# One block for attention and its inputs, and key and query loads in 12 transfers in place of 20

## The reference, cut to what matters

```python
h = layernorm(x) * (1 + ca) + sa                   # ca, sa: rows of silu(c) @ wmod
Xn = (h - mu) * rsqrt(var + 1e-5) * ln_g + ln_b
Q, K, V = split_heads(Xn @ Wq + bq), split_heads(Xn @ Wk + bk), split_heads(Xn @ Wv + bv)
A = softmax(where(causal, Q K^T / 4, -inf))        # 16 heads of 16 channels, 512 tokens
x = x + ga * ((A V) @ Wo + bo)
```

## Time and profile before

| | |
|---|---|
| median of 3 runs | 1178.86 us (1175.69 to 1179.64) |
| the profiled execution, its own time | 1173.97 us |
| its span, first to last instruction | 1171.9 us |
| mean granted TensorE clock | 0.897 |
| first attention scores / last attention values | 118.4 us / 362.0 us |
| busy share TensorE, VectorE, ScalarE, GpSimd | 81%, 63%, 56%, 39% |

### The profile page before, as it was taken

The page is one execution under the profiler, slowest core; times in us unless marked ns, Lnnn a source line. Parts: engine busy times, 40 slices in busy tenths (PEclk is TensorE's granted clock), DMA queues, the critical chain, the costliest instruction groups (busy, mean ns, idle before and its releaser), DMA issues. The chain is left out here.

```text
span 1171.9 us, 21496 instructions
## 1 busy us (share of the span) xinstructions
PE 954.3 (81%) x5454; PEld 796.3 (68%) x5454; DVE 742.1 (63%) x1917; ACT 652.3 (56%) x1693; POOL 456.9 (39%) x637
## 2 busy tenths in 40 slices
PE   6671999999997767969999970689699974999992
PEld 2461788888886655758999960468487753888882
DVE  4870798999994676468555535996447773444444
ACT  3562898999993345458666642579533322333331
POOL 3373564666662177603444443576301121010000
PEclk9786898999998787979999995799899986999997
DMA  7066443343322522447343429310042203000004
GB/s 247 17 222 212 114 102 90 91 90 90 90 54 64 180 100 101 153 150 251 124 128 121 126 98 303 99 45 1 14 143 75 72 28 127 24 31 33 28 15 152
DMA packets 112107, 123.15 MB, mean 105 GB/s; under 512 B 46720, under 2 KB 85120, under 8 KB 111896
## 3 DMA queue, kind: packets, MB, share of 16 engines
q1 hardware_dynamic: 102584, 97.89, 28.4%
q0 software_dynamic: 8608, 23.20, 5.3%
q10 hardware_dynamic: 832, 1.05, 0.3%
HBM read 77.73 MB, written 44.35 MB: 104 GB/s over the span
## 5 line engine op out<-in xcount | busy, mean ns | idle before, releaser
L717 ACT ACTIVATE PR<-PS,nmax 128x128 f32<-128x128 f32 (+3 forms) x256 | 135.7, 553 | 9.7 <-DVE nmax L758 8.4
L758 DVE TENSOR_REDUCE nmax<-PS 128x1 f32<-128x128 f32 (+3 forms) x256 | 113.5, 481 | 42.4 <-PE PS L661 37.0
L635 POOL TENSOR_SCALAR PR<-PR,rinv 128x128 f32<-128x128 f32 (+3 forms) x256 | 132.3, 537 | 0.0
L1355 POOL DMA_INDIRECT r_results<-r_y,r_to x79 | 75.9, 961 | 111.8 <-DVE r_to L1410 76.8
L660 PE MATMUL PS<-K,Q 128*128 128x128 f32 (+3 forms) x256 | 84.6, 390 | 30.4 <-PEq L138 26.4
L766 DVE TENSOR_TENSOR PTlo<-PS,PThi 128x512 fp32r<-128x512 f32 (+1 forms) x192 | 103.0, 590 | 2.9 <-ACT PThi L727 2.9
L727 ACT ACTIVATE PThi<-PS 128x512 fp32r<-128x512 f32 (+1 forms) x192 | 97.0, 547 | 6.7 <-PE PS L673 6.7
L673 PE MATMUL PS<-ident,PR 128*128 128x128 f32 x640 | 86.7, 281 | 3.6 <-DVE PTlo L766 3.0
L689 PE MATMUL PS<-PThi,V 128*128 128x512 f32 (+3 forms) x256 | 85.3, 346 | 1.1 <-DVE PTlo L766 0.5
L2350 DVE TENSOR_TENSOR x_h<-PS,x_sg 128x256 f32<-128x256 f32 x68 | 28.9, 424 | 86.4 <-ACT x_sg L2304 86.4
L2304 ACT ACTIVATE x_sg<-PS 128x256 f32<-128x256 f32 x68 | 26.2, 385 | 95.2 <-PE PS L2444 95.2
(11 more groups left out here) (374 smaller groups left out, 3067.8 us busy)
## 6 DMA issues: line engine op xcount, KB each, us to landing
r_xg<-r_sorted SPq DMA_DIRECT2D x79, 129.0 KB
r_wst<-in_routed SPq DMA_DIRECT2D x16, 608.0 KB, 5.3
K<-k_parts SPq DMA_DIRECT2D x120, 64.0 KB, 1.8
v_parts<-vp SPq DMA_DIRECT2D x4, 1024.0 KB, 7.5
V<-v_parts SPq DMA_DIRECT2D x64, 64.0 KB, 2.1
mlp_st<-r_results SPq DMA_DIRECT2D x8, 512.0 KB, 7.9
c_yg<-r_results SPq DMA_DIRECT2D x8, 512.0 KB
mlp_st<-in_up SPq DMA_DIRECT2D x8, 512.0 KB, 3.7
```

Source lines behind the costliest of these rows:

```text
L635: pool.tensor_scalar(PR[:, e % 4, i, 0:w], PR[:, e % 4, i, 0:w], rinv[:, e % 4, i:i + 1], 1.0, ALU.mult, ALU.mult).then_inc(norm_done, 1)
L717: act.activation(PR[:, e % 4, i, 0:w], k.PS[:, i, 0:w], ACT.Exp, bias=nmax[:, e % 4, i:i + 1], accum_out=rsum[:, e % 4, i:i + 1]).then_inc ...
L758: dve.tensor_reduce(nmax[:, e % 4, i:i + 1], k.PS[:, i, 0:P * (i + 1)], AX_X, ALU.max, negate=True).then_inc(max_done, 1)
L1355: pool.indirect_dma_start(out=d.results, out_offset=bass.IndirectOffsetOnAxis(ap=to[:, i % TO_LANES:i % TO_LANES + 1], axis=0), in_=y[:, i ...
```

## The change

The two blocks become one: `attention_inputs` returns a program for each engine, and `attention` calls it ahead of its own part. No engine waits for all others between the two. `qhi`, `qlo` and `vp` get a second buffer for odd batches, in the place of `wm`. SP now stores batches 0 and 1, loads tiles 0 and 1 whole, stores batch 2, loads tile 2's keys once tile 0's scores are made, and stores batch 3; ScalarE loads nothing. GpSimd issues the row stores between its other steps (`store_rows`), and ScalarE waits for them at the end of its inputs. TensorE, before its first scores, waits for the last evictions. A tile's keys and queries come in 12 transfers: each names both copies as a source with a leading dimension of 2.

```diff
+            store(0)
+            store(1)
             sp.wait_ge(heads.zeroed, 4)
-            for b in range(B):
-                store(b)
-            for i in range(1, len(ROW_SETS)):
-                sp.wait_ge(k.rows_out[i], 16)
+            heads.wait_stored(sp, 0)
+            for u in range(2):
+                heads.load_keys(sp, 0, u, u)
+                heads.load_values(sp, 0, u, u)
+            store(2)
+            sp.wait_ge(heads.s_ready, 16)
+            heads.load_keys(sp, 0, 2, 0)
+            store(3)
...
+            def store_rows(b):
+                for i in ((1,), (2,), (3, 4), (5,))[b]:
+                    pool.wait_ge(row_done, i + 1)
+                    pool.dma_start(k.mod_rows[i], row[:, i, :]).then_inc(k.rows_out[i], 16)
...
             def queries(j):
                 def stage(b):
                     act.wait_ge(q_ready, b * 4 + j + 1)
+                    if b >= 2:
+                        act.wait_ge(q_out[j][b % 2], b // 2 * 32)
                     if b:
-                        act.wait_ge(q_out[j], b * 32)
+                        act.wait_ge(qlo_done, (b - 1) * 4 + j + 1)
...
-            def first_keys(b):
-
-                if b >= 2:
-                    act.wait_ge(heads.zeroed, 4)
-                    heads.wait_stored(act, 0)
-                    heads.load_keys(act, 0, 0, 0, range(2 * b - 4, 2 * b - 2))
...
+            for i in range(1, len(ROW_SETS)):
+                act.wait_ge(k.rows_out[i], 16)
...
+            pe.wait_ge(q_done, B * 4 * 2)
+            pe.wait_ge(vf_done, B * 2)
...
-    def load_keys(self, sp, b, q, u, heads=range(4)):
-
-        for s in heads:
+    def load_keys(self, sp, b, q, u):
+
+
+        for s in range(4):
             r = 64 * (s % 2)
-            src = self.k.k_parts[b, q, s].rearrange("a r t -> (a r) t")
-            for dup in range(2):
-                sp.dma_start(f32(self.K4[u][r + 32 * dup:r + 32 * dup + 32, s, :]), src).then_inc(self.k_in[u], 16)
-            src = self.k.q_parts[b, q, s]
-            sp.dma_start(f32(self.Q4[u][r:r + 32, s // 2, :]), src.rearrange("a r t -> (a r) t")).then_inc(self.q_in[u], 16)
-            for dup in range(2):
-                sp.dma_start(f32(self.Q4[u][r + 32 + 16 * dup:r + 48 + 16 * dup, s // 2, :]), src[1 - dup]).then_inc(self.q_in[u], 16)
+            for a in range(2):
+                src = self.k.k_parts[b, q, s, a].unsqueeze(0).to_broadcast([2, DH, T])
+                sp.dma_start(f32(self.K4[u][r + 32 * a:r + 32 * a + 32, s, :]), src).then_inc(self.k_in[u], 16)
+            src = self.k.q_parts[b, q, s].rearrange("a r t -> (a r) t").unsqueeze(0).to_broadcast([2, 2 * DH, T])
+            sp.dma_start(f32(self.Q4[u][r:r + 64, s // 2, :]), src).then_inc(self.q_in[u], 16)
...
         @block.sync
         def _(sp):
-
-            heads.load_keys(sp, 0, 1, 1)
-            for u in range(2):
-                heads.load_values(sp, 0, u, u)
...
+            inputs.sync(sp)
...
             def pair(it, b, qp):
                 for u in range(2):
...
-            pair(1, 0, 1)
+                    keys(it, b, qp, u)
+                values(it, b, qp)
+            keys(1, 0, 1, 1)
+            values(1, 0, 1)
             heads.wait_stored(sp, B - 1)
             out_weights.load(sp, wo)
```

More of the change, by code:

```diff
@@ L1 @@
+from collections import namedtuple
 from contextlib import ExitStack
@@ L210, in store @@
                     dst = (k.q_parts, k.k_parts)[j // 2]
-                    for part, tile in enumerate((qhi, qlo)):
+                    for part, tile in enumerate((qhi[b % 2], qlo[b % 2])):
                         sp.dma_start(dst[b, 2 * (j % 2):2 * (j % 2) + 2, :, part].rearrange("q s r t -> (q s) r t"),
-                                     f32(tile[:, j, :])).then_inc(q_out[j], 16)
+                                     f32(tile[:, j, :])).then_inc(q_out[j][b % 2], 16)
                 sp.wait_ge(vhi_done, (b + 1) * 2)
@@ L265, in values_lo, with scalar @@
                     for t in (2 * g, 2 * g + 1):
-                        last = pool.tensor_tensor(vp[:, t, :, 1, :], vf[:, t, :].rearrange("p (h d) -> p h d", d=DH),
-                                                 f32(vp[:, t, :, 0, :]), ALU.subtract)
+                        last = pool.tensor_tensor(vp[b % 2][:, t, :, 1, :], vf[:, t, :].rearrange("p (h d) -> p h d", d=DH),
+                                                 f32(vp[b % 2][:, t, :, 0, :]), ALU.subtract)
                     last.then_inc(vlo_done, 1)
[L269 to L275, removed]
+            wavefront((8, values_lo), (0, root(0)), (4, zero), (5, root(1)), (7, queries(0)), (7, queries(1)), (7, queries(2)), (7, queries(3)), (6, store_rows))
+        def scalar(act):
             act.wait_ge(c_in, 16)
@@ L336, in values, with vector @@
                     for t in (2 * g, 2 * g + 1):
-                        last = act.activation(vp[:, t, :, 0, :], vf[:, t, :].rearrange("p (h d) -> p h d", d=DH), ACT.Copy)
+                        last = act.activation(vp[b % 2][:, t, :, 0, :], vf[:, t, :].rearrange("p (h d) -> p h d", d=DH), ACT.Copy)
                     last.then_inc(vhi_done, 1)
-            def first_keys(b):
-                if b >= 2:
-                    act.wait_ge(heads.zeroed, 4)
-                    heads.wait_stored(act, 0)
-                    heads.load_keys(act, 0, 0, 0, range(2 * b - 4, 2 * b - 2))
             wavefront((2, columns), (3, queries(0)), (3, queries(1)), (3, queries(2)), (0, first_norm), (0, evict), (1, weights), (1, second_norm),
-                      (3, queries(3)), (3, values), (3, first_keys))
-        @block.vector
-        def _(dve):
+                      (3, queries(3)), (3, values))
+            for i in range(1, len(ROW_SETS)):
+                act.wait_ge(k.rows_out[i], 16)
+        def vector(dve):
             own = Chain(dve, own_dve)
@@ L466, in _, with tensor @@
                       (4, lo), (4, modulations), (5, values))
-        @block.tensor
-        def _(pe):
+        def tensor(pe):
             pe.wait_ge(silu_done, 1)
@@ L580, in load, with attention @@
                              wo.rearrange("(q h r) n -> h r q n", q=QUADS, h=4)[h]).then_inc(self.w_in, 16)
-def attention(k, heads, OT, out_weights, wo):
+def attention(k, inputs, heads, OT, out_weights, wo):
     nc = k.nc
@@ L604, in _, with keys, values @@
         def _(sp):
-            heads.load_keys(sp, 0, 1, 1)
-            for u in range(2):
-                heads.load_values(sp, 0, u, u)
[L610 to L614, removed]
+            inputs.sync(sp)
+            def keys(it, b, qp, u):
+                sp.wait_ge(s_ready, it * 32 - 16 + 16 * u)
+                heads.load_keys(sp, b, qp * 2 + u, u)
+            def values(it, b, qp):
                 for u in range(2):
@@ L618, in pair @@
                     heads.load_values(sp, b, qp * 2 + u, u)
-            pair(1, 0, 1)
+            def pair(it, b, qp):
+                for u in range(2):
+                    keys(it, b, qp, u)
+                values(it, b, qp)
+            keys(1, 0, 1, 1)
+            values(1, 0, 1)
             heads.wait_stored(sp, B - 1)
@@ L746, in body @@
                         hi(2)
+            inputs.scalar(act)
             loop(act, body)
```

74 lines of the change are left out of this document (40 added, 34 removed).

## The result

The changed kernel takes **1342.18 us** (median of 4 runs, 1337.85 to 1344.28) against 1177.28 for the kernel before (median of 4, 1173.41 to 1179.64): a ratio of 1.140 with a 95% interval of 1.135 to 1.145. The forecast was 1325 with a range of 1290 to 1390. The profiled execution took 1344.28 us with a span of 1342.6; the forecast for that execution was 1320.

What follows compares the result with a forecast made beforehand. Two DMA queues were to bound attention: 83 us until free plus 396.2 of transfers puts tile 15 at 479.2, not 337.21 (+142.0); with slow start and late values +146 on 1178.86 gives 1325 us, range 1290 to 1390.

Steps and rivals of the forecast that it cites:

- Two engines, the same two: Key and query loads, source 2 rows outermost, all 12 a tile on the same 2 of 16 DMA engines.
- Rivals 1 and 2: Loads spread as before (1150 us, 8%), or two engines but others for each transfer (1152 us, 3%).
- rival 1: Loads spread by the destination's partitions: 2.7 us a tile, hidden, border and tile 4 gains won, 1150 us; 8%.
- 84 ns a piece: Engine time for each 2 KB piece of keys and queries, with 80 and 118 ns kept as ends.
- Rival 4: A 2 KB piece costs 118 ns in place of 84: +150 us, 1475 us; 6%.
- 23.1 us a tile: Attention loads: keys and queries 21.5 us on two engines plus values 1.6, against TensorE's 14.4 us a tile.
- The values' term: A tile's value loads on 16 engines: 128 packets an engine at 13 ns, 1.6 us.
- so none: No gaps in the two queues: SP issues tile n+2 within 17 us of n landing, n+1 lands after 23.1.
- Tile 0 at 105.5: First scores of attention: engines free at about 83, plus 21.5 for tile 0's loads and 1 of landing, about 106.
- 4.1 (slow start, late values): Added at tile 15: slow start 2.1 us, and about 2 waiting for tile 14's values behind tile 15's keys.
- rival 3: TensorE's clock drops after each tile's idle time, whole tiles slow at 24.6 us: +35 us, 1360; 10%.
- The 24 us of the border and the 5 of tile 4 are inside this.: Earlier attention start (24 us) and tile 4's shorter issues (5 us) shorten a path that no longer ends last.

Runs made afterwards that it cites:

- twelve_on_sixteen: Changed kernel, still 12 loads a tile, but the copy moved inward so the rows are outermost: 1162.19 us, ratio 0.988 to the kernel before.
- one_value_load: Changed kernel with only the values of each tile's first head loaded, the other three left out: 1306.61 us.
- keys_on_two: Changed kernel with keys loaded as in the change but queries as two transfers of 32 rows, 16 loads a tile: 1201.4 us.
- store_three_in_halves: store_three_between with store 3 split over two places in SP's program and Wo put between the values of tiles 6 and 7: 1155.47 us.
- blocks_before_twelve_on_sixteen: Kernel before, its two blocks kept, with the 12 loads of twelve_on_sixteen: 1170.38 us, ratio 0.996.
- merged_old_loads: Changed kernel, blocks merged, with the 20 loads a tile of the kernel before: 1172.06 us, ratio 0.998.
- store_three_between: loads_before_stores with store 3 moved between the keys of tiles 6 and 7, Wo behind tile 7's keys: 1161.02 us.
- stores_on_sixteen: Merged block with high and low parts in separate DRAM halves, stores 128 rows outermost, 16 loads a tile: 1164.36 us.
- loads_before_stores: twelve_on_sixteen with tile 2's keys ahead of store 2, and store 3, then Wo, after the loads of tiles 4 and 5: 1169.44 us.

## Why the prediction was right, and where its sum was off

**Two engines, the same two.** Right: 13.1% of sixteen and 49 GB/s with keys and queries alone in flight, where "near 0.15" and "some 50" stood. Over all of attention the share was 0.19 to 0.20, at 55 to 57 GB/s. The forecast's own terms give that and not 0.15: two of sixteen engines for 21.5 us and all of them for 1.6, in 23.1 us, are 0.19. The share of 0.52 for stores with 8 rows outermost was enough to read it from. Rivals 1 and 2 (loads spread) fell with the first queue view; twelve_on_sixteen shows that loads spread over more engines are hidden behind TensorE, as rival 1 said, once the rows are outermost.

**84 ns a piece.** Right: 83.3 with only these in flight, and 43.36 us for 512 pieces in one_value_load. Rival 4 (118 ns) fell. By the packet records of the kernel before, half of the 2 KB pieces in the stretch of the earlier trace rows took 84 ns or less too; a tail of long ones, up to 0.3 us, made the mean. Choosing 84 was right, and why some pieces are long there no run tells.

**23.1 us a tile.** 1.0 low, at 24.1. The values' term was mis-sized: priced at 1.6 us a tile by their bytes, they cost 2.6, because the two engines run dry for a while ("so none" was the answer to "are there gaps?"). The step looked for gaps in when SP is allowed to issue a tile, and not in how long SP takes to issue. From tile 5 to tile 15 (260.65 to 501.51) it is 240.9 us in place of 231: +9.9. A slip beside it: 14 tiles' values at 1.6 us are 22.4, and the sum has 22.9.

**Tile 0 at 105.5.** It came at 111.4, 5.9 late. SP issued store 1's values at 81.66 and not 79.66, 2.0 of them; the other 3.9 were not taken apart.

**Tiles 1 to 5.** 149.3 us from tile 0 to tile 5 where the sum has 142.7 for its part, +6.6. The same stretch was priced too low in keys_on_two. The largest loss that the trace shows in it is again a queue run dry: tile 4's keys were issued at 214.69, behind eight value loads and eight loads of Wo, and from 207.1 to 216.2 us no piece of 2 KB is in flight. SP's timeline:

```profile
195.93 13.07 SPq L584 DMA_DIRECT2D V<-v_parts  x8
209.37 4.92 SPq L595 DMA_DIRECT2D wo_st<-in_wo  x8
214.69 1.47 SPq L578 DMA_DIRECT2D K<-k_parts  x2
```

What stores 2 and 3 add to it was not measured apart.

These three make 9.9 + 5.9 + 6.6, which is 22.3 before rounding, and the sum's 479.2 plus 22.3 is the 501.5 of the trace. For the rest of attention the forecast had added 4.1 (slow start, late values); from tile 15's start to the next block it is 2.4 longer than before (501.51 to 530.55, against 337.21 to 363.88). The stages behind, priced at 0, are 4.0 longer, which no run explains; but from TensorE's first product behind attention to the end the thirteen traces lie between 805.7 and 811.4 us, so this may be no more than how one execution differs from the next. Together 22.3 - 4.1 + 2.4 + 4.0 = 24.6, the 24 us between 1320 and 1344.

**The clock (rival 3).** Half there, and harmless. The mean granted clock fell to 0.76 to 0.81 in attention, but a tile's work, 13.9 to 17.0 us of it, still ends before the next tile's keys are in (TensorE waits at every tile), so it can have added little before tile 15. Its deciding point, a tile of slow work over about 20 us, was not reached.

**"The 24 us of the border and the 5 of tile 4 are inside this."** Right for the changed kernel. But rival 1's time, 1150, was wrong, and so is the reason given for it: with loads on sixteen engines the kernel takes 1162.19, a gain of 12.6 us and not 29. The cost of the changed order in SP was priced as "SP's wait for tile 0's scores has store 3 queued behind it ... nobody waits for store 3 itself". Nobody does, but tile 3's keys stand behind it, as the chances noted for 1%, and tile 2's behind store 2, which the text missed. It took three orders to get from 1162.19 to 1155.47, by the ratios about 5 us.

## What to carry to other kernels

Before folding several transfers into one, write down the outermost dimension of both sides: in these runs a copy dimension of 2 placed outermost cost 170 us and the copy placed inside cost nothing, at the same count of transfers. The sign of it here was a low DMA share beside an engine that waits for DMA. And when blocks are merged, one queue's program becomes the order of everything in it: read it for each load that stands behind work nobody waits for, and time where the issues themselves have room.

## What the runs showed of the hardware that was not expected

**A backlog on two engines slows the issuer, for transfers over all sixteen too.** With the backlog on two DMA engines, SP took 13.47 us to issue eight value loads that take 4.44 us in twelve_on_sixteen (146.69), and a pair of 64 KB key loads took up to 4.85 where 1.44 was enough when the queue was short (285.44 and 315.88). The Trainium skill (DMA: Bandwidth & Descriptors, "Rules for kernel authors") says that a leading broadcast of c copies confines a transfer to at most c engines; the share of 13.1% agrees. No run here shows which two engines these are.

**Two waits of 1.3 us, and 5.7 us lost.** In store_three_in_halves TensorE waits 1.35 us before tile 3 and 1.27 in its first head. Stages of 121 to 155 us (the PE clock is third from the end):

```profile
121.00:136.00 15.00, 13.90 (x102) 11.75 (x101) 14.36 (x34) 14.21 (x47) 9.70 (x22) 1.00 0.64 209
136.00:140.00 4.00, 2.46 (x10) 2.02 (x11) 2.74 (x7) 2.83 (x10) 1.18 (x4) 0.68 0.76 119
140.00:146.00 6.00, 6.00 (x33) 5.42 (x31) 2.43 (x6) 3.36 (x11) 1.76 (x4) 0.64 0.45 135
146.00:155.00 9.00, 8.84 (x69) 7.53 (x67) 8.59 (x22) 8.03 (x26) 5.47 (x14) 1.00 0.12 39
```

The clock, at its upper level (2.4 GHz) until 136 us, has a mean of 0.68 and 0.64 in the ten microseconds after, so part of them is at the lower level (1.2 GHz), although TensorE is busy all of 140 to 146. The tile takes 18.3 us where the next takes 14.0. With the wait ahead of it that is 5.7 us lost; the two waits are 2.6 of them, and an estimate by the difference leaves 3.1 for the clock. After the waits of 4.53 and 4.45 us in twelve_on_sixteen it was granted 0.50 for the first 3.5 us. Not every small wait is followed by this. After single waits of 1.17 us in blocks_before_twelve_on_sixteen and 1.03 in merged_old_loads, both before tile 4, the clock stayed at 1.00 and the tile took 13.7 to 13.8 us; after the wait of 1.53 us for values in this kernel (at 171.02) it stayed at 1.00 too. Where a second wait followed in the tile's first head, it fell: 1.21 and 1.3 us in store_three_between, 1.54 and 1.71 in stores_on_sixteen, 1.43 and 1.17 in loads_before_stores, all before tile 3. So a late transfer can be paid for twice; that it takes the second wait is what these traces suggest, and no run tests it alone.
